# A selective-scan kernel: two quarters of B's diagonals are built by VectorE instead of GpSimd

## The reference, cut to what matters

```python
def step(h, inp):
    u_t, d_t, B_t, C_t = inp
    dA = jnp.exp(d_t[..., None] * As)
    h = h * dA + (d_t * u_t)[..., None] * B_t[:, :, None, :]
    y = jnp.einsum('bkcn,bkn->bkc', h, C_t)
    return (h, y)
```

## Time and profile before

| | us |
|---|---|
| median of 3 runs (lowest, highest) | 1742.99 (1727.37, 1746.87) |
| the profiled execution | 1741.23 |
| its span, first to last instruction | 1739.2 |
| scan stage, from its first scan to its last | 239 to 1380 |
| granted TensorE clock, mean of the span | 0.91 of full speed |

### The profile page before, as it was taken

The page is one execution under the profiler, slowest core; times in us unless marked ns, Lnnn a source line. Parts: engine busy times, 40 slices in busy tenths (PEclk is TensorE's granted clock), DMA queues, the critical chain, the costliest instruction groups (busy, mean ns, idle before and its releaser), DMA issues. The chain is left out here.

```text
span 1739.2 us, 66737 instructions
## 1 busy us (share of the span) xinstructions
PE 1408.3 (81%) x30536; PEld 866.9 (50%) x30536; DVE 1268.6 (73%) x1082; ACT 983.4 (57%) x1900; POOL 1094.1 (63%) x346
## 2 busy tenths in 40 slices
PE   7798467886977879787697887778868759989998
PEld 5643254554644545455464554545545325635565
DVE  4893149899797898978889898797999884352311
ACT  3323377777777778676787777767776221211212
POOL 0144039998988889888798898988989840020000
PEclk8996559999999999999999999999999977867989
DMA  9225033333322333323243332333323350100101
GB/s 324 112 119 217 12 72 88 98 86 87 99 73 82 103 82 104 93 63 85 69 116 92 84 101 74 92 86 88 86 82 82 123 224 1 53 20 4 69 28 46
DMA packets 59463, 157.39 MB, mean 90 GB/s; under 512 B 17046, under 2 KB 25750, under 8 KB 58672
## 3 DMA queue, kind: packets, MB, share of 16 engines
q1 hardware_dynamic: 59184, 153.13, 29.6%
HBM read 104.86 MB, written 35.65 MB: 81 GB/s over the span
## 5 line engine op out<-in xcount | busy, mean ns | idle before, releaser
L962 POOL TENSOR_TENSOR s_h<-s_h,s_crow 128x2048 f32<-128x2048 f32 (+1 forms) x256 | 879.9, 3467 | 172.0 <-DVE s_h L930 171.9
L930 DVE TENSOR_TENSOR_SCAN s_h<-s_a,s_pb 128x1024 f32<-128x1024 f32 x384 | 864.6, 2277 | 153.8 <-PE s_py L757 79.5
L734 PE MATMUL s_pb<-k_area,s_dtut 64*64 64x64 f32 x24576 | 472.6, 225 | 207.6 <-DVE s_h L930 163.9
L734 PEld LDWEIGHTS s_pb<-k_area,s_dtut 64*64 64x64 f32 x24576 | 426.9, 138 | 405.7 <-DVE s_h L930 232.6
L838 ACT ACTIVATE s_a<-s_dup,s_aneg 128x1024 f32<-128x1024 f32 x384 | 437.4, 1140 | 54.7 <-DVE s_h L930 54.6
L757 PE MATMUL s_py<-s_h,k_eye 64*64 64x512 f32 x3072 | 424.1, 607 | 28.1 <-ACT y_y L844 15.6
L822 ACT ACTIVATE k_area<-k_mask,s_bt 128x64 f32<-128x64 f32 x1024 | 281.4, 337 | 0.0
L622 POOL TENSOR_TENSOR k_area<-s_bt,k_mask 128x2048 f32<-128x2048 f32 x32 | 139.2, 4351 | 31.4 <-ACT s_bt L797 31.4
L757 PEld LDWEIGHTS s_py<-s_h,k_eye 64*64 64x64 f32 x3072 | 90.9, 137 | 40.2 <-issue 16.0
L1303 POOL TENSOR_TENSOR t_gated<-t_yt,t_sz 128x256 f32<-128x256 f32 x16 | 13.2, 822 | 118.4 <-DVE t_yt L1349 118.4
L814 ACT ACTIVATE s_pm<-y_y 128x512 f32<-128x512 f32 x48 | 28.6, 596 | 103.9 <-DVE y_y L906 103.8
(11 more groups left out here) (158 smaller groups left out, 1374.6 us busy)
## 6 DMA issues: line engine op xcount, KB each, us to landing
s_crow<-scratch_xd SPq DMA_DIRECT2D x256, 256.0 KB, 4.1
s_dup<-s_dup SPq DMA_DIRECT2D x48, 256.0 KB, 3.6
k_area<-in_x_dram SPq DMA_DIRECT2D x4, 1536.0 KB, 8.5
scratch_xt<-h_xt SPq DMA_DIRECT2D x4, 1536.0 KB, 10.7
scratch_ub<-h_xb SPq DMA_DIRECT2D x12, 512.0 KB, 2.6
y_y<-scratch_y SPq DMA_DIRECT2D x4, 1536.0 KB, 11.1
k_area<-scratch_xt SPq DMA_DIRECT2D x4, 1536.0 KB, 9.0
out_dram<-t_out SPq DMA_DIRECT2D x32, 192.0 KB, 1.9
```

The source lines that it names most:

```text
L734: mm = pe.matmul(pb[par * HALF:(par + 1) * HALF, step % 2, r * BANK + blk:(r + 1) * BANK:BLK], dtut[here, u % 2, blk, g * HALF:(g + 1) * H ...
L930: nc.vector.tensor_tensor_scan(h[:, step % (TRIPLES * CG), f], a[:, step % RING, f], pb[:, step % 2, f], 0.0, ALU.mult, ALU.add).then_inc( ...
L962: nc.gpsimd.tensor_tensor(here, here, c.unsqueeze(1).broadcast_to([P, groups.stop - groups.start, L]), ALU.mult).then_inc(hc_ready, 1)
```

## The change

Pieces 1 and 3 are built by VectorE with the same operation and the same operands. Piece 3 comes behind the scan of step 3 of the unit, piece 1 of the next unit behind that of step 18; piece 1 of unit 0 is built ahead of the first scan. GpSimd keeps nothing but the merged products in the scan stage. The semaphore d_pool is renamed d_dve; its counts stay.

```diff
@@ TensorE, spread_b
                 if i % 6 == 0:
                     piece = i // 6
-                    pe.wait_ge(d_pool if piece % 2 else d_act, 2 * u + piece // 2 + 1)
+                    pe.wait_ge(d_dve if piece % 2 else d_act, 2 * u + piece // 2 + 1)
@@ ScalarE, take_chunk
                 if what == "BT":
                     need(act, d_act, 2 * (u - 1))
-                    need(act, d_pool, 2 * (u - 1))
+                    need(act, d_dve, 2 * (u - 1))
@@ VectorE
             times_u(0)
+            build_d(dve, nc.vector.tensor_tensor, 0, 1, d_dve)
             for u in range(UNITS):
...
                         if i == 15:
                             times_u(u + 1)
+                        if i == 18:
+                            build_d(dve, nc.vector.tensor_tensor, u + 1, 1, d_dve)
+                    if i == 3:
+                        build_d(dve, nc.vector.tensor_tensor, u, 3, d_dve)
@@ GpSimd
             pool.wait_ge(shared["kept_in"], 16 * len(KEPT))
-            build_d(pool, nc.gpsimd.tensor_tensor, 0, 1, d_pool)
             for u in range(UNITS):
                 for n in range(NP):
                     times_c(u * NP + n, range(0, 2))
                     times_c(u * NP + n, range(2, CG))
-                    if n == 1:
-                        build_d(pool, nc.gpsimd.tensor_tensor, u, 3, d_pool)
-                    if n == 4 and u + 1 < UNITS:
-                        build_d(pool, nc.gpsimd.tensor_tensor, u + 1, 1, d_pool)
```

More of the change, by code:

```diff
@@ L596, in scan @@
         d_act = sem("d_act")
-        d_pool = sem("d_pool")
+        d_dve = sem("d_dve")
         a_ready = sem("a_ready")
```

## The result

The changed kernel is slower: median 1780.4 us of 4 runs (1767.8 to 1791.4) beside 1744.9 us before, ratio **1.0259** (95% interval 1.0197 to 1.0322). The ratios in this document leave out executions more than 1.5% above the fastest of the same kernel, and they are not the quotient of the two medians. Times 1742, the ratio is 45 us (34 to 56 by its interval); the two medians are 35 us apart. The forecast was 45 us over the median shown (1788 against 1743). The profiled execution has a span of 1785.4 us.

The account below looks back on a forecast made before the run. The prediction took a loop between VectorE and TensorE in the scan stage as the bound, not GpSimd. Build 3 (22 us) and build 1 (24 us) sum to 46 us, giving 1788 us, range 1764 to 1820.

Parts of the forecast that it names:

- GpSimd does not bound the kernel: Scan stage: no one is held up by GpSimd, so relieving it of 32 builds is worth zero.
- A build costs 2.18 us of queue: VectorE's queue: each build of 2048 columns takes 2.18 us; 31 among scans, 68 us if nothing hides them.
- The wait for the port: VectorE's builds may wait for a whole GpSimd product: 0.65 to 0.85 us behind step 3, 0.17 behind step 18.
- won races: Behind step 18 VectorE asks 0.1 us before GpSimd's second product; the rival of losing: 1823 us, chance 0.12.
- The rival without it: Rival that builds never wait for the port: 32 us more, 1774 us, chance 0.15.
- Build 3: Piece 3 behind step 3 delays TensorE's step 6: 1.4 us in odd units, 2.4 in some even ones; 22 us.
- The cover in units 4, 8, 12: TensorE waits 5.19 us there for ScalarE to take y, hiding build 3: zero cost, otherwise 2.4 us each.
- Build 1: Piece 1 behind step 18 delays the scan of step 21 by a mean 1.6 us: 15 x 1.6 = 24 us.
- what could swallow part of the sum: TensorE's 34.6 us of "issue" stalls could swallow some of the forecast or the no-port-wait rival, down to 1762 us.
- The sum: Whole kernel: 22 + 24 = 46 us more, forecast 1788 us, 2.6% slower, chance 0.6.
- Hidden altogether: Rival that VectorE's idle time in steps 0 to 8 hides all builds: about 1743 us, chance 0.07.
- Faster: Rival that GpSimd's builds delay products and adds: 1731 or 1670 us; chance 0.03 for more than 1%.

Follow-up runs that it names:

- The trial of the relief: Kernel before without GpSimd's builds after unit 0 (TensorE reads unit 0's pieces), nothing added to VectorE: 0.9946, on another chip 1.0088.
- Trials 3 to 5: Changed kernel with build 1 behind step 17: 1.0552; build 1 twice behind step 18: 1.0624; builds behind steps 4 and 16: 1.016, 1 and 4: 1.0096.
- piece 1 alone: Kernel before with only piece 1 built by VectorE, behind step 18; piece 3 stays on GpSimd: 1.0086.
- piece 3 alone: Kernel before with only piece 3 built by VectorE, behind step 3; piece 1 stays on GpSimd: 1.0157.
- steps 1 and 4: Changed kernel with both pieces built in their own unit, piece 1 behind step 1, piece 3 behind step 4: 1.0096.
- trial 3: Changed kernel with build 1 behind step 17 instead of 18: 1.0552 times the kernel before.
- trial 8: GpSimd's products cut to 64 of 1024 columns, in the changed kernel: 1.0251, and in the kernel before: 1.0269.
- its trial with cut products: Changed kernel with GpSimd's merged products cut to 64 of 1024 columns: 1.0251 times the kernel before.
- trial 7: Kernel before with times_u moved to GpSimd and both builds on VectorE behind steps 1 and 4: 1.0181.

## Why the prediction held, point by point

- **GpSimd does not bound the kernel.** Right in the profile: TensorE's matmuls waited 0.6 us for products and its weight loads 2.3 us, and GpSimd's waits took all its relief. The trial of the relief gave 0.9946 and 1.0088, which shows no gain but is too coarse to show an exact zero.
- **A build costs 2.18 us of queue.** 2.27 us long, the next scan 2.18 us behind its start where no product is in the way (324.45 to 326.63). Right.
- **The wait for the port.** Behind step 3, predicted 0.65 to 0.85 us; builds of 2.73 to 3.25 us in 13 of 16 units, so 0.5 to 1.0; none in units 0 and 7. Behind step 18, predicted 0.17 us and won races; 2.33 us long in all 15 units, so 0.06, all won. In unit 15 the build waited 1.8 us, where I had put its cost at 2.0 us in all; steps 3 to 9 took 4.1 more. Trials 3 to 5 show that the wait is there, that it is one whole instruction, and that the place decides it. The rival without it is out.
- **Build 3: the term of the sum that was too small.** Predicted 22 us, measured 31.6 in the stretch of the changed kernel and 26.9 alone. The sum had no term for TensorE's clock. Units 1, 3 and 13 give +1.5, +1.3 and +1.4 us for a predicted 1.4, and unit 7, whose build met no product, +0.6. Units 5, 9 and 11 give +3.1, +2.9 and +2.9. The rows of TensorE at step 6 tell the two kinds apart: the 64 matmuls and the adds take 1.16 and 1.07 us in units 1, 3, 7 and 13, but 1.98 and 1.96 in unit 5, 1.49 and 2.00 in unit 9, 1.33 and 2.00 in unit 11. That is 1.7, 1.3 and 1.1 us more, for surpluses of 1.7, 1.5 and 1.5. Units 2, 6, 10 and 14 give +3.1 to +4.0 for 2.4. There the clock is not the whole answer: in unit 2 step 6 runs at 1.16 and 1.07 us, its build waited 1.0 instead of 0.65 us, and behind `take_y` the kernel before has slow matmuls too. The rest of their surplus stays open. The cover in units 4, 8, 12 held (-0.3 to -0.8).
- **Build 1: the term that was too large.** Predicted 24 us, measured 13.0 and 14.7. The waits came as forecast: from step 18 to the next step 0 of units 0 to 14, TensorE's `spread_b` waits for scans 31.4 us instead of 7.2, which is 24 more. But its "issue" stalls in the same stretch fell from 16.9 to 8.2 us. The trials isolate this: they are 8.9 us with piece 1 alone on VectorE, and 19.6 and 17.3 us in the two trials without a build on VectorE in this stretch (piece 3 alone, and steps 1 and 4). So the wait for the build covers stalls that were there anyway, some 8 to 9 us of the 9 to 11 by which the term was too large. I had named them as what could swallow part of the sum, but left them out of the middle.
- **The sum.** 22 + 24 = 46 us; the stage gave +37 in the profile, the ratios 27 + 15 = 42 and 45, the medians 35. The mechanism held; that the total came so close is luck, since two errors of some 10 us each and of opposite sign cancelled.
- **The other rivals.** Hidden altogether: out at 1.0259, though behind step 4 in odd units it is just what happens. Faster: out.

## What to carry to other kernels

Before moving work to the faster engine, ask who waits for the slower one: here nobody did, and the profitable move was the reverse, 1.65 us a unit off the queue that is full onto the one that waits (0.9844; 20 us in the stretch concerned). An operation that shares a port with a neighbour must be placed by the neighbour's timetable: the same build cost 2.27, 2.33, 3.2 or 4.75 us behind steps 4, 18, 3 and 17, and one step later in the loop made it free in odd units. A trial that shortens one engine's work shifts all that follows on it, and can bring about a new meeting; read the durations of everything that shares its port before taking it as a bound.

## What the runs showed of the hardware

The port is held for whole instructions (the 2.6 us of waiting in trial 3), and it also works against VectorE when GpSimd's operation is a build (`times_u` 2.23 instead of 1.73 us in trial 8). That whoever issues first gets the shared pair for the whole instruction, while the other fully blocks, is also the rule of the Trainium skill (SBUF — State Buffer, Who interferes with whom). The 4.75 us of trial 3 agree with it.

The tail, with the same code in all kernels, took 346 to 375 us, the longer the lower TensorE's granted clock. Three windows, from the last scan on: the changed kernel, then its trial with cut products, then trial 7 (PEclk is the third number from the right):

```profile
1417.00:1785.00 368.00, 330.20 (x1160) 188.85 (x1152) 142.92 (x357) 71.28 (x114) 34.91 (x37) 0.79 0.15 54
```

```profile
1413.00:1759.00 346.00, 309.04 (x1156) 182.71 (x1152) 140.36 (x357) 71.33 (x114) 32.03 (x36) 0.84 0.15 57
```

```profile
1382.00:1757.00 375.00, 332.54 (x1160) 189.15 (x1160) 141.81 (x358) 71.22 (x114) 39.73 (x37) 0.78 0.14 53
```

The last two ran on the same chip. That is 29 us between executions, more than most effects looked for here. Where a change lies in one stage, the span of that stage in the trace says more than one total time.
